# Attention layer with masked heads: layer-1 keys in quarters two head pairs ahead, guards from step 2, mask rows in 32 pieces, one matmul row for both heads' maxima

## The reference, cut to what matters

```python
keys    = einsum('nj,hjk->hnk', h, Wks)      # 8 heads of 64
queries = einsum('nj,hjk->hnk', h, Wqs)
values  = einsum('nj,hjk->hnk', h, Wvs)
atts = einsum('hqk,hmk->hqm', queries, keys) / 8
atts = atts - 1e16 * (1 - max(adj, eye))     # adj: 4096 x 4096, f32
atts = softmax(atts, axis=-1)
x = x + einsum('hqm,hmk,hko->qo', atts, values, Wo)
```

## Time and profile before

| | us |
|---|---|
| median of 3 runs | 5021.12 |
| lowest, highest | 5012.50, 5022.32 |
| the profiled execution's own time | 5012.62 |
| span of the profiled execution | 5010.9 |
| PE busy | 4584.9 (91%) |
| POOL busy | 3452.4 (69%) |
| DVE busy | 3379.6 (67%) |
| ACT busy | 3110.1 (62%) |
| mean granted TensorE clock | 0.965 of 2.4 GHz |

### The profile page before, as it was taken

How to read it: one execution, slowest core, us unless ns; L and a number is a source line. 1 busy time by engine, 2 the same in 40 slices (tenths; PEclk the granted TensorE clock), 3 DMA queues, 4 the chain that set the end, 5 groups by cost and what they waited for, 6 DMA issues and landing times.

```text
span 5010.9 us, 128860 instructions
## 1 busy us (share of the span) xinstructions
PE 4584.9 (91%) x43282; PEld 2220.7 (44%) x43793; DVE 3379.6 (67%) x6969; ACT 3110.1 (62%) x5768; POOL 3452.4 (69%) x2969
## 2 busy tenths in 40 slices
PE   5679999999999878699999899999999999999998
PEld 2322222222222234245555555555555555555555
DVE  6868888888888633556656556557557557466565
ACT  3345555555555333167777677677687687677675
POOL 1157776676777500078878788788788788788786
PEclk8789999999999989789999999999999999999999
DMA  7743233233232234453523425325244334334334
GB/s 310 311 115 97 87 109 93 91 111 93 92 108 70 92 100 118 149 131 91 150 74 110 131 73 139 99 77 156 78 109 134 86 101 135 93 98 130 92 100 120
DMA packets 354936, 583.29 MB, mean 116 GB/s; under 512 B 31200, under 2 KB 219648, under 8 KB 337088
## 3 DMA queue, kind: packets, MB, share of 16 engines
q1 hardware_dynamic: 348992, 557.63, 37.4%
q0 software_dynamic: 5120, 16.78, 1.1%
q10 hardware_dynamic: 128, 0.13, 0.0%
HBM read 497.61 MB, written 76.82 MB: 115 GB/s over the span
## 4 chain that ended last, share of the span: by engine, by line
PE 37%; issue 4%; DMA 3%; SPq 3%; DVE 2%; ACT 1%; POOL 1%; DVEq 0%; ACTq 0%; POOLq 0%
PE d_gd L1475 9%; PE d_sc L1490 6%; PE d_sc L1491 6%; PE d_sc L1492 5%; PE d_acc L1509 3%; PE d_acc L1511 3%; PE d_acc L1519 3%; DMA d_KA<-scratch_kl 3%; PE d_misc L1534 2%; POOL d_PL L1264 1%; SPq L1152 1%; DVE d_junk L1359 1%; ACT d_PH L1305 1%; ACT d_PF L1301 1%; SPq L1153 1%
## 5 line engine op out<-in xcount | busy, mean ns | idle before, releaser
L1264 POOL TENSOR_TENSOR d_PL<-d_PF,d_PH 128x512 f16<-128x512 f32 x2048 | 2357.0, 1176 | 630.6 <-ACT d_PH L1305 628.3
L1359 DVE CUSTOM_DVE_ANT_0 d_junk<-d_gd,d_MR 128x512 bf16<-128x512 f32 x2112 | 1445.0, 690 | 779.2 <-PE d_gd L1475 712.2
L1301 ACT ACTIVATE d_PF<-d_sc 128x512 f32<-128x512 f32 x2048 | 1234.0, 603 | 767.4 <-remote 385.1
L709 DVE SCALAR_TENSOR_TENSOR b_P<-b_R,u,b_A 128x512 f32<-128x512 f32 x1792 | 1202.4, 743 | 217.8 <-ACT b_A L621 154.8
L1305 ACT ACTIVATE d_PH<-d_sc 128x512 f16<-128x512 f32 x2048 | 1239.6, 605 | 0.0
L750 PE MATMUL b_acc<-b_P,V 128*64 128x512 f32 x4096 | 943.2, 601 | 38.1 <-DVE b_P L709 25.3
L1475 PE MATMUL d_gd<-d_KA,d_QA 128*128 128x512 f16 x2112 | 817.7, 387 | 135.6 <-DVE d_gm L1359 47.5
L1490 PE MATMUL d_sc<-d_QA,d_KA 128*128 128x512 f16 x2048 | 783.6, 383 | 64.9 <-ACT d_PH L1305 37.3
L1491 PE MATMUL d_sc<-d_QL,d_KB 128*128 128x512 f16 x2048 | 781.8, 382 | 0.0
L1511 PE MATMUL d_acc<-d_V,d_PH 128*128 128x64 f16 x8192 | 643.4, 194 | 0.0
L1509 PE MATMUL d_acc<-d_V,d_PH 128*128 128x65 f16 x8192 | 642.4, 193 | 0.1
(11 more groups left out here) (128 smaller groups left out, 3916.5 us busy)
## 6 DMA issues: line engine op xcount, KB each, us to landing
d_stage<-in_adj SPq DMA_DIRECT2D x144, 512.0 KB, 4.3
d_V<-scratch_v SPq DMA_DIRECT2D x131, 520.0 KB, 4.3
a_rows<-in_adj SPq DMA_DIRECT2D x32, 2048.0 KB, 9.5
b_stage<-in_adjT SPq DMA_DIRECT2D x128, 512.0 KB, 3.6
d_MT<-scratch_mt SPq DMA_DIRECT2D x36, 1024.0 KB, 6.3
d_KA<-scratch_kh SPq DMA_DIRECT2D x66, 512.0 KB, 8.1
d_KA<-scratch_kl SPq DMA_DIRECT2D x66, 512.0 KB, 10.2
d_KB<-scratch_kh SPq DMA_DIRECT2D x264, 128.0 KB, 3.0
```

Of the source, the lines that this page charges most:

```text
L709: nc.vector.scalar_tensor_tensor(out=PT[:, m % P_STEPS, h, :], in0=R[:, par, h, :], scalar=T["u"][:, m, h:h + 1], in1=A[m % A_RING][:, :], ...
L1264: eng.tensor_tensor(PL[:, t % H_RING, :], PF[:, t % F_RING, :], PH[:, t % H_RING, :], ALU.subtract).then_inc(s_lowp if by_pool(t) else s_l ...
L1301: nc.scalar.activation(PF[:, t % F_RING, :], sc[t % 2][:, :], ACT.Exp, scale=EXP_SCALE)
L1359: nc.vector.tensor_tensor_reduce(out=junk[:, gi % 2, :], in0=gd[gi % 2][:, :], in1=MR[:, s, c * QB:(c + 1) * QB], scale=1.0, scalar=-3.0e3 ...
```

## The change

Keys of layer 1 are loaded in four parts of 1024 columns, each as soon as the running pair has used that part of its own keys, for the pair two further on (which uses the same buffer). Guards wait part by part, and run over steps 2 to 28. The last quarter of MT is loaded at step 10 of the block that uses it instead of at the end of the block before. Mask pieces are 512 wide, 32 a block, in six staging buffers of half the size. The maxima of both heads are turned together: four matmuls with two columns each into two rows, and DVE's copy multiplies each row by 0 or 1 so that each head's QL takes its own.

```diff
--- before.py
+++ after.py
@@ -1024,15 +1024,16 @@
     GUARDS = 2 * SUB * MC
-    CW = 1024
+    CW = 512
     CH = N // CW
...
     MASK_OPS = 2 + SUB * ROW_OPS
-    FIRST_G, LAST_G = 5, 28
+    FIRST_G, LAST_G = 2, 28
     CROW_STEP = 30
-    S_RING = 3
+    MT_LATE = 10
+    S_RING = 6
     K = D + 1
@@ -1048,7 +1049,7 @@
     FIRST_C = (HP - 2) * NT + 12
-    CHUNK_STEPS = [FIRST_C + 5 * ci // 2 for ci in range(CHUNKS)]
+    CHUNK_STEPS = [FIRST_C + 5 * ci // 4 for ci in range(CHUNKS)]
     SETUP_STEP, DIAG_STEP = FIRST_C - 1, FIRST_C - 9
@@ -1095,8 +1096,9 @@
         cm = sb("d_cm", [P, 2, SUB])
-        cmh = sb("d_cmh", [P, 2, SUB], F16)
+        cmh = sb("d_cmh", [P, SUB, 2], F16)
         shift = sb("d_shift", [P, 1])
+        only = sb("d_only", [P, 2])
         idh = sb("d_idh", [P, P], F16)
@@ -1108,7 +1110,7 @@
         s_set = sem("constants_set")
-        s_KA = [[sem(f"ka_in{i}{x}") for x in range(2)] for i in range(2)]
+        s_KA = [[sem(f"ka_in{par}{i}") for i in range(GROUPS)] for par in range(2)]
         s_Q = [sem(f"q_in{i}") for i in range(2)]
@@ -1139,11 +1141,12 @@
-        def load_ka(sp, par, hp):
+        def load_ka(sp, par, hp, i):
+            cols = slice(i * PER * P, (i + 1) * PER * P)
             for x in range(2):
                 row = (2 * hp + x) * D
-                sp.dma_start(KA[0:D, par, x, :], DR["kh"][row:row + D, :]).then_inc(s_KA[par][x], 16)
-                sp.dma_start(KA[D:P, par, x, :], DR["kl"][row:row + D, :]).then_inc(s_KA[par][x], 16)
+                sp.dma_start(KA[0:D, par, x, cols], DR["kh"][row:row + D, cols]).then_inc(s_KA[par][i], 16)
+                sp.dma_start(KA[D:P, par, x, cols], DR["kl"][row:row + D, cols]).then_inc(s_KA[par][i], 16)
@@ -1189,12 +1192,15 @@
                 load_chunk(sp, 0, ci)
-            load_ka(sp, 0, 0)
             load_q(sp, 0, 0, 0)
+            for i in range(GROUPS):
+                load_ka(sp, 0, 0, i)
             for ci in range(S_RING, CHUNKS):
...
                 load_chunk(sp, 0, ci)
+            for i in range(GROUPS):
+                load_ka(sp, 1, 1, i)
             for i in range(GROUPS):
@@ -1215,13 +1221,15 @@
                             load_q(sp, par, nxt, nb if hp < HP - 1 else (nb + 1) % NB)
-                            load_ka(sp, par, nxt)
                         if mb % PER == PER - 1:
...
                             sp.wait_ge(s_S, nb * TILES + (hp * PAIR + 2 * (mb + 1) + CREDIT))
+                            load_ka(sp, hp % 2, (hp + 2) % HP, mb // PER)
                             load_kb(sp, nxt, mb // PER)
-                            if hp == HP - 1:
+                            if hp == HP - 1 and mb < NT - 1:
                                 load_mt(sp, (nb + 1) % NB, mb // PER)
+                        if step == MT_LATE and not first:
+                            load_mt(sp, nb, GROUPS - 1)
                         if mb % PER == LAG:
@@ -1250,13 +1258,13 @@
             for par in range(2):
-                for x in range(2):
-                    sp.wait_ge(s_KA[par][x], 32 * (2 * NB + 1 - par))
+                for i in range(GROUPS):
+                    sp.wait_ge(s_KA[par][i], 64 * (2 * NB + 1))
                 sp.wait_ge(s_Q[par], 96 * (2 * NB + 1 - par))
...
                 sp.wait_ge(s_V[i], 16 * (HP * NB + (1 if i < GROUPS - 1 else 0)))
-                sp.wait_ge(s_MT[i], 16 * (NB + 1))
+                sp.wait_ge(s_MT[i], 16 * (NB + (1 if i < GROUPS - 1 else 0)))
@@ -1275,7 +1283,7 @@
             act.wait_ge(s_const, 16 * 2)
-            act.wait_ge(s_set, 5)
+            act.wait_ge(s_set, 6)
             act.sem_inc(s_P, CREDIT)
@@ -1314,8 +1322,9 @@
             dve.wait_ge(s_set, 2)
-            nc.vector.memset(KB[D:D + 1, :, :], C_ROW).then_inc(s_set, 1)
-            nc.vector.memset(shift[D:D + 1, :], P_SHIFT / C_ROW).then_inc(s_set, 1)
+            nc.vector.memset(KB[D:D + 2, :, :], C_ROW).then_inc(s_set, 1)
+            nc.vector.memset(shift[D:D + 2, :], P_SHIFT / C_ROW).then_inc(s_set, 1)
+            nc.vector.tensor_copy(only[D:D + 2, :], T["identf"][D:D + 2, D:D + 2]).then_inc(s_set, 1)
             nc.vector.tensor_scalar(idm[:, :], T["identb"][:, :], -MASK_FLOOR, None, ALU.mult).then_inc(s_set, 1)
@@ -1363,14 +1372,14 @@
                     dve.wait_ge(s_cm, it + 1)
-                    nc.vector.tensor_scalar(cmh[:, :, :], cm[:, :, :], -1.0 / C_ROW, None, ALU.mult).then_inc(s_cmh, 1)
+                    nc.vector.tensor_scalar(cmh[:, :, :].rearrange("p s x -> p x s"), cm[:, :, :], -1.0 / C_ROW, None, ALU.mult).then_inc(s_cmh, 1)
...
+                dve.wait_ge(s_crow, it + 1)
                 for x in range(2):
-                    dve.wait_ge(s_crow, it * 2 + (x + 1))
-                    nc.vector.tensor_scalar(QL[D:D + 1, par, x, :], gd[x][D:D + 1, :], shift[D:D + 1, :], None,
-                                            ALU.add).then_inc(s_crowc, 1)
+                    nc.vector.tensor_scalar(QL[D:D + 2, par, x, :], gd[0][D:D + 2, :], shift[D:D + 2, :], only[D:D + 2, x:x + 1],
+                                            ALU.add, ALU.mult).then_inc(s_crowc, 1)
@@ -1412,10 +1421,10 @@
                 mask_chunk(0, 0, ci)
-                for gi in range(4 * (ci - CH), 4 * (ci - CH) + 4):
+                for gi in range(2 * (ci - CH), 2 * (ci - CH) + 2):
                     if gi >= 0:
                         guard(0, gi, 2 + ROW_OPS * (gi // (2 * MC) + 1) if gi % (2 * MC) == 0 else None)
-            for gi in range(4 * (CHUNKS - CH), GUARDS):
+            for gi in range(2 * (CHUNKS - CH), GUARDS):
                 guard(0, gi, MASK_OPS if gi % (2 * MC) == 0 else None)
@@ -1443,8 +1452,9 @@
                             mask_setup(nb + 1, (nb + 1) % NB)
-                        if step in CHUNK_STEPS:
-                            mask_chunk(nb + 1, (nb + 1) % NB, CHUNK_STEPS.index(step))
+                        for ci in range(CHUNKS):
+                            if step == CHUNK_STEPS[ci]:
+                                mask_chunk(nb + 1, (nb + 1) % NB, ci)
@@ -1458,28 +1468,28 @@
             pe.wait_ge(s_const, 16 * 2)
-            pe.wait_ge(s_set, 5)
+            pe.wait_ge(s_set, 6)
             pe.sem_inc(s_S, CREDIT)
...
                 s, x, c = gi // (2 * MC), gi // MC % 2, gi % MC
-                if s == 0 and c == 0:
-                    if x == 0:
-                        pe.wait_ge(s_Q[par], count * 96 + 96)
-                    pe.wait_ge(s_KA[par][x], count * 32 + 32)
+                if gi == 0:
+                    pe.wait_ge(s_Q[par], count * 96 + 96)
+                if s == 0 and x == 0 and c % (MC // GROUPS) == 0:
+                    pe.wait_ge(s_KA[par][c // (MC // GROUPS)], count * 64 + 64)
                 if gi >= 2 or not isinstance(it, int):
...
-            def crow(it, x):
+            def crow(it):
...
                 for s in range(SUB):
-                    mm = nc.tensor.matmul(gd[x][D:D + 1, s * P:(s + 1) * P], cmh[:, x, s:s + 1], idh[:, :], start=True, stop=True,
+                    mm = nc.tensor.matmul(gd[0][D:D + 2, s * P:(s + 1) * P], cmh[:, s, :], idh[:, :], start=True, stop=True,
                                           tile_position=(0, D))
@@ -1546,8 +1556,7 @@
                 guard(0, 0, gi, 0)
-            for x in range(2):
-                crow(0, x)
+            crow(0)
@@ -1556,8 +1565,8 @@
                             pe.wait_ge(s_Q[hp % 2], count * 96 + 96)
-                            for x in range(2):
-                                pe.wait_ge(s_KA[hp % 2][x], count * 32 + 32)
+                            for i in range(GROUPS):
+                                pe.wait_ge(s_KA[hp % 2][i], count * 64 + 64)
@@ -1573,8 +1582,7 @@
                         if mb == CROW_STEP:
-                            for x in range(2):
-                                crow(it, x)
+                            crow(it)
```

## The result

The changed kernel takes 5113.31 us in the median (5109.60 to 5123.00, 4 runs), the kernel before 5020.63 beside it (5012.50 to 5022.32, 4 runs). The ratio is 1.0193, 95% interval 1.0179 to 1.0207: slower by 93 us, where 47 was forecast; the median lies 8 us above the forecast range of 5030 to 5105. The profiled execution took 5114.87 us (span 5113.2), its mean granted clock is 0.954 against 0.965.

A forecast was written before the change was run, and what follows sets the result against it. PE sets the pace where it has guard matmuls and POOL where it has none. Query waits 122 us plus half clock 37, minus gains 112, give +47 us on 5021: 5068 us, 0.9% slower, range 5030 to 5105.

The forecast's parts named there:

- The query wait takes the place of the key wait: First guard of each pair: waits for the last query transfer instead of keys; the forecast case, 5048 to 5092 us, chance 0.62.
- Together 122 us: PE idle for queries at pair entries: 56 us into pairs 1 and 2, 34 into pair 3, 32 into pair 0.
- 2.4 us: SP at step 31: four key transfers at 0.59 us go ahead of the KB and query transfers.
- 24 x 0.85 x 1.35: Half clock behind the query wait at entries into pairs 1 to 3: costs 28 us.
- The spread of the guards: Guards over steps 2 to 28 fill PE time that steps 2 to 4 waste: 0.72 us, 31 times, gain 22 us.
- Mask pieces ... gain 30: Guards' weight loads behind DVE: half pieces of 0.89 us fit better, a third of the 45.5 us wait kept.
- Row of the maxima: Turning the maxima: four fewer matmuls in each of 32 pairs, gain 7 us.
- Start of the layer ... Gain 4: Layer 1's start: seventh mask piece lands near 2092.5, guards start some 3 us earlier, gain 4 us.
- The keys' 49: Layer-1 key waits of PE go: 38.1 us of waits, 4.4 uncounted idle, 6.8 half clock; gain 49 us.
- The clock did not hold: Rival at pairs 1 to 3: clock holds behind the query wait, 28 us go, 5040 us; chance 0.12.
- Masks did not get worse: Rival on DVE's mask pieces: each half piece costs 1.26 us, wait doubles to 91, 5144 us; chance 0.07.
- The rival on the other side, queries nearly there: Rival at the first guard: 1.5 us idle without clock loss, faster at 4955 us; chance 0.13.

The follow-up runs named there:

- Experiment 1: Changed kernel with the six query transfers issued at step 31 ahead of the keys, for the pair two further on; both banks loaded first: 4946.33 us, ratio 0.9859.
- experiment 4: Changed kernel with four more small transfers into a spare buffer between the last key quarter and KB: 5206.94 us in one execution.
- experiment 3: Changed kernel with 56 matmuls of 128 columns, result unused, ahead of the first guard's wait for the queries: 5073.52 us, ratio 1.0113.
- experiment 2: Changed kernel with guards over steps 5 to 28 again, order of the loads kept: 4969.22 us, ratio 0.9899.
- experiment 5: Kernel before with mask rows in 32 half-width pieces and six staging buffers, nothing else: 4990.25 us, ratio 0.9938.
- experiment 7: Experiment 1 with mask rows in 16 pieces of 1024 and three staging buffers again: 4949.09 us, ratio 0.9857.
- experiment 8: Changed kernel with queries issued first and both heads in one transfer for key, KB and query loads: 4939.13 us, ratio 0.9839.
- experiment 10: Kernel before with its guards from step 2 and nothing else: 5244.99 us, ratio 1.0450.

## Why the prediction was right in direction and short in size

The steps that failed are sizes: of the 46 us between forecast and measurement, 23 are the query wait, 11 the half clock, and 12 are gains that fell short.

**Right: the mechanism.** The query wait takes the place of the key wait, at the first guard of every pair, with half clock behind it. Experiment 1 changes only the order of the loads and moves the time by 167 us; experiment 4 makes the wait longer on purpose and the time follows.

**Mis-sized: the query wait, "Together 122 us".** The trace has 139.7, and 145 with the 0.17 us that the prediction adds for each wait (32 times, 5.4). By its terms: pairs 1 and 2 took 4.6 us where it had 3.5 (74 for 56), pair 3 took 5.6 for 4.2 (45 for 34), pair 0 took 2.8 for 4.6 (20 for 32), and the layer's first pair 6.6 for nothing. Two steps failed. "2.4 us" for four key transfers and the six query issues as in the earlier trace rows assumed the old pace; the eleven issues ahead of the last took 7.8 us (3344.46 to 3352.24) instead of 6.9, as one issue in it took 1.28. And "some 31 waits" left out the initial list, whose order I read for the mask pieces alone: pair 1's queries are its last entry. In pair 0 the error had the other sign: two entries stood for seven.

**Mis-sized: the half clock, "24 x 0.85 x 1.35".** All 24 entries of pairs 1 to 3 show it, for 3.4 or 6.8 us, and it costs about 2.0 us each (experiment 3, pairs 1 and 2): 48 us for 28. The upper end of the prediction's own bounds was 1.7, worked out for a single stretch of 3.4 us.

The two together fit: experiment 1 takes 167 us away and leaves 22 of wait (26 with 0.17 for each of 25), so the whole is 193 = 145 + 48, where 159 stood (122 + 37). What the half clock of pair 0 costs, put at 9, can't be told here from that of the loop's end, which was there before.

**The gains, "= 112 us".** 193 - 93 = 100 remained of them. The spread of the guards and the mask pieces were put at 22 + 30 = 52; experiments 1 and 2 differ by 23 us, and by 46 once their query waits (26 and 3) are taken out. The size of that sum was nearly right and its attribution wrong: "Mask pieces ... gain 30" belongs to the spread, which the step itself named beside the width (experiments 5 and 7). Row of the maxima: 7 forecast, 6 measured. "Start of the layer ... Gain 4" did not come: the load of the seventh piece went out at 2093.4 instead of 2089.5 and DVE stood until 2097.7. The first scores came at 2155.6 after 2154.2 before; kernels with the same start had them between 2149.7 and 2155.6, so the sign of this is not settled.

The keys' 49 can't be separated well. Step 5, where the first guard stands both before and in experiment 2, fell there from 3.35, 3.58 and 3.93 us in pairs 1 to 3 to 2.92, which is 17 us, and in pair 0 from 7.92 to 2.95, which is 35. The sum is what the term says. But experiment 2 has only 50 us less than the kernel before, 6 of it the maxima; more than half lies in pair 0, which got 4.0 us shorter (97.6 for 101.6), and experiment 5 shows that pair 0 shortens by as much when SP's loop end happens to cost little, with the keys where they were. The 17 are the keys' own; how much of the 35 is stays open.

**The rivals.** The clock did not hold at any of the 24 entries of pairs 1 to 3; in pair 0 it fell behind the query wait in four of seven, and the other three show only the half clock of the loop's end. Masks did not get worse. The rival on the other side, queries nearly there, asked for an idle of 1.5 us with the clock up; experiment 1 made one of 0.9 (22.2 in 25), at 4946 us where the rival had 4955.

## What to carry to other kernels

When a consumer is moved ahead, list every input it waits for and the place of each in the order of issues: here two inputs share a queue, and advancing one pushed the other back. In one queue, what is due first goes first, and what has a whole pair of time goes last; merging transfers took 4.1 us off the issue here and put 3.1 on the landing. Behind each idle of 3.9 to 6.0 us in pairs 1 to 3 PE ran at half clock, which cost 2 us on top of the wait. And where a long instruction of another engine falls decides more than its width: step 9 of pair 3, with a mask piece and the diagonal, takes 4.2 us with three guards, where 2.67 is usual, and with two the usual 2.46. Look at who released the wait before naming it; step 4 of experiment 8 had the look of a late load and was a mask piece.

## Not expected of the hardware

In most bursts of issues on SP, one took 1.0 to 1.8 us instead of 0.6 (1.28 and 1.52 in the rows above); which one changed from kernel to kernel, and no run here tells why. The end of SP's loop took about 5.5 us less in experiment 5 than in the kernel before, from code that differs on SP only in the loads of the mask. An issue costs SP 0.60 us for 128 KB as for 256 KB. The half clock came in lengths of 3.4 and 6.8 us, and of 10.2 us in experiments 4 and 10, whose waits were the longest, and at some loop ends.
